# Transposes of the attention probabilities, issued one behind each score matmul instead of in a row

## The reference, cut to what matters

```
scores = (q_nope @ k_nope.T + q_pe @ k_pe.T) * 192 ** -0.5
scores = where(mask, scores, -inf)          # mask: the 128 best causal keys of each query
attn   = softmax(scores, axis=-1)
out    = attn @ v                           # then @ o_w, added to x
```

## Time and profile before

| | us |
|---|---|
| median of 3 runs (896.3 to 898.85) | 897.53 |
| span of the profiled execution | 897.2 |
| first attention pass, about | 300 to 500 of the span |
| second attention pass, about | 500 to 801 of the span |
| a unit of the second pass, from one O to the next | 18.79 |
| PE busy over the span | 805.0 (90%) |
| DVE busy over the span | 675.8 (75%) |

### The profile page before, as it was taken

The page is one execution under the profiler, slowest core; times in us unless marked ns, Lnnn a source line. Parts: engine busy times, 40 slices in busy tenths (PEclk is TensorE's granted clock), DMA queues, the critical chain, the costliest instruction groups (busy, mean ns, idle before and its releaser), DMA issues.

```text
span 897.2 us, 20231 instructions
## 1 busy us (share of the span) xinstructions
PE 805.0 (90%) x7496; PEld 500.7 (56%) x7496; DVE 675.8 (75%) x1557; ACT 596.7 (67%) x1340; POOL 531.0 (59%) x440
## 2 busy tenths in 40 slices
PE   4979989977777988898988899999999999999998
PEld 2445544444344655565555567777767777764443
DVE  5365677789998989999999788888888888861000
ACT  2656789978886878787887676776666767750000
POOL 3185368876884555545545587888878788840000
PEclk9989999999998999999999999999999999999999
DMA  8012211112333444443443288788778777880110
GB/s 254 24 36 74 80 41 54 58 31 85 105 114 89 130 125 115 131 111 111 136 129 105 65 137 167 135 137 155 149 147 147 141 137 152 165 168 15 68 51 32
DMA packets 168786, 96.67 MB, mean 108 GB/s; under 512 B 116720, under 2 KB 142704, under 8 KB 168688
## 3 DMA queue, kind: packets, MB, share of 16 engines
q1 hardware_dynamic: 168688, 95.37, 45.8%
HBM read 36.62 MB, written 6.29 MB: 48 GB/s over the span
## 4 chain that ended last, share of the span: by engine, by line
PE 28%; POOL 22%; DVE 21%; issue 15%; DMA 5%; SPq 4%; ACT 4%; POOLq 0%; DVEq 0%; ACTq 0%
PE psS L773 9%; DVE m L1176 5%; DMA arena<-arena 4%; DVE bias L1183 4%; DVE arena L1042 3%; DVE arena L1236 3%; SPq L451 3%; PE psS L700 3%; PE psT L572 2%; PE psT L552 2%; PE psS L529 2%; POOL arena L1356 2%; POOL arena L1469 2%; POOL bias L1422 2%; ACT arena L804 2%
## 5 line engine op out<-in xcount | busy, mean ns | idle before, releaser
L804 ACT ACTIVATE arena<-psT 128x512 f16<-128x512 f32 (+4 forms) x360 | 171.9, 506 | 107.0 <-PE psT L757 67.1
L700 PE MATMUL psS<-keyT,arena 128*128 128x512 f16 (+3 forms) x1152 | 232.6, 330 | 5.2 <-issue 3.0
L1236 DVE CUSTOM_DVE_ANT_0 arena<-psS,bias 128x512 f32<-128x512 f32 (+7 forms) x256 | 191.9, 751 | 36.7 <-PE psS L700 17.0
L991 ACT ACTIVATE arena<-arena,small 128x512 f32<-128x512 f32 (+7 forms) x256 | 197.5, 774 | 31.0 <-DVE small L1236 30.1
L1042 DVE SCALAR_TENSOR_TENSOR arena<-psT,arena 128x512 f16<-128x512 f32 (+3 forms) x278 | 146.1, 545 | 26.3 <-ACT arena L804 25.7
L757 PE MATMUL psT<-ident,arena 128*128 128x128 f32 x736 | 117.3, 281 | 26.3 <-DVE arena L1042 24.3
L700 PEld LDWEIGHTS psS<-keyT,arena 128*128 128x128 f16 x1152 | 92.6, 99 | 57.1 <-issue 8.1
L585 PE MATMUL psS<-ikT,big 128*128 128x512 f16 (+3 forms) x528 | 102.8, 339 | 23.9 <-DVE bias L1127 20.0
L757 PEld LDWEIGHTS psT<-ident,arena 128*128 128x128 f32 x736 | 86.1, 143 | 59.1 <-ACT arena L991 32.3
L1422 POOL TENSOR_TENSOR bias<-arena,bias 128x768 f32<-128x768 f32 (+2 forms) x48 | 91.4, 1918 | 32.7 <-ACT arena L870 22.3
L1183 DVE MATCH_REPLACE8 bias<-m,bias 128x768 f32<-128x768 f32 (+4 forms) x112 | 89.9, 809 | 0.0
(11 more groups left out here) (164 smaller groups left out, 1387.2 us busy)
## 6 DMA issues: line engine op xcount, KB each, us to landing
arena<-arena SPq DMA_DIRECT2D x192, 128.0 KB, 2.4
arena<-in_wiq SPq DMA_DIRECT2D x32, 256.0 KB, 2.7
arena<-in_ow SPq DMA_DIRECT2D x16, 512.0 KB, 3.5
arena<-in_qbT SPq DMA_DIRECT2D x16, 256.0 KB, 2.5
wvo_parts<-arena SPq DMA_DIRECT2D x16, 256.0 KB, 2.0
arena<-in_qpe SPq DMA_DIRECT2D x16, 128.0 KB, 3.0
arena<-in_x SPq DMA_DIRECT2D x8, 256.0 KB, 3.2
out<-arena SPq DMA_DIRECT2D x8, 256.0 KB, 2.0
```

Of the source, the lines that this page charges most:

```text
L700: last = mm(bank[:, k:k + w], Q[:, u % 2, h, a, q:q + P], keyT[:, b, h, k:k + w], start=(a, b) == (0, 0), stop=(a, b) == (1, 0))
L804: return nc.scalar.activation(dst, src, ACT.Copy, scale=scale)
L991: nc.scalar.activation(pr[:, g % 4, 0:kw], pr[:, g % 4, 0:kw], ACT.Exp, bias=shift[:, g % 4:g % 4 + 1], scale=-1.0, accum_out=rsum[:, unit ...
L1236: v.tensor_tensor_reduce(out=pr[:, g % 4, 0:kw], in0=bank[:, 0:kw], in1=bias[:, TOFF[t]:TOFF[t + 1]], scale=-c_s, scalar=3e38, op0=ALU.add ...
```

## The change

In the second pass, for even steps g that have a step g + 3, the transposes of g are no longer issued in a row behind the six score matmuls of step g + 3. One is issued behind each of these matmuls, and what is left over (3 of 8, none of 5, 1 of 7) follows behind the sixth; of these the first stands behind the score matmul that raises `s_mm`. The waits for `exp_done` and for the two banks of the ring go with the first and the fifth transpose. This holds for 63 steps: four in each of the 16 units, without step 6 of the last one. The first pass keeps its order. The instructions of DVE, ACT, POOL and SP, and their order, stay as they are.

```diff
-            def scores(g):
+            def scores(g, between=None):
 ...
-                last.then_inc(s_mm, 1)
+                        if (a, b) == (1, 0) and k + w == kw:
+                            last.then_inc(s_mm, 1)
+                        if between:
+                            turn_block(between, next(between[1], None))
+
+            def turn_block(step, j):
+
+                if j is None:
+                    return
+                g, nb = step[0], tile_of(step[0]) + 1
+                c = j // 4
+                use = ("T", g, c)
+                if j == 0:
+                    pe.wait_ge(exp_done, g + 1)
+                if j % 4 == 0:
+                    wait_freed(BEFORE[use])
+                last = nc.tensor.transpose(psT[BANK[use]][:, (j % 4) * P:(j % 4 + 1) * P],
+                                           pr[:, g % 4, j * P:(j + 1) * P], ident[:])
+                if j % 4 == 3 or j == nb - 1:
+                    last.then_inc(t_mm, 1)
 ...
             for g in range(STEPS):
+                blocks = iter(range(0 if turns(g) else tile_of(g) + 1))
                 if g + AHEAD < STEPS:
-                    scores(g + AHEAD)
-                if not turns(g):
-                    pe.wait_ge(exp_done, g + 1)
+                    scores(g + AHEAD, (g, blocks) if half_of(g) and not turns(g) else None)
+                for j in blocks:
+                    turn_block((g, blocks), j)
                 for use in uses_of(g):
                     what, at, c = use
                     bank = psT[BANK[use]]
+                    if what == "T":
+                        continue
                     wait_freed(BEFORE[use])
-                    if what == "T":
-                        for j in range(4 * c, min(4 * c + 4, tile_of(g) + 1)):
-                            last = nc.tensor.transpose(bank[:, (j % 4) * P:(j % 4 + 1) * P],
-                                                       pr[:, g % 4, j * P:(j + 1) * P], ident[:])
-                        last.then_inc(t_mm, 1)
-                    elif what == "O":
+                    if what == "O":
```

## The result

The changed kernel takes 910.04 us in the median (909.4 to 911.59), the kernel before 897.39 beside it: a ratio of 1.0146, 95% interval 1.0131 to 1.0161, so 12.6 us slower. The forecast was 908.5, in a range of 899 to 914.

The account below looks back on a forecast made before the run. PE was taken to set the pace, busy 18.65 of 18.79 us a unit. 13 x 0.72 = 9.4, plus 1.1 and 0.55, made 11.0 on a span of 897.2; with 0.3 for the median, 908.5, range 899 to 914.

Parts of the forecast that it names:

- Nothing to win on PE: Transposes between score matmuls on PE: each still costs 0.109 us, as in a row, so alternating is worth nothing.
- `s_mm` late by 0.545: In odd steps `s_mm` comes five transposes later, 5 x 0.109 = 0.545 us, delaying DVE's `row_max` and what queues behind it.
- The hole ahead of O: PE's wait for DVE before O, once a unit: grows from 0.30 to 0.84 us.
- L and the fifth transpose: PE waits 0.18 us at L; step 6's fifth transpose, dependent on DVE's read of L, is due at about that lateness.
- The two waits are one and the same lateness: Step 6's fifth transpose adds no wait beyond L's 0.18 us; the sixth score matmul starts 0.72 later.
- the 13 regular units: Units of the second pass with the full delay: 0.72 us each, 9.4 us together.
- The first unit: First unit of the second pass: taken like the last but one, with only the first step's 0.545 us coming through.
- The three end terms: Second pass's first and last but one units, 1.1 us together, and its last unit, 0.55 us.
- A: Rival for PE: a transpose behind a score matmul costs 0.056 instead of 0.109 us, giving 883 us; chance 0.08.
- C: Rival for PE: each change between fp32 and half precision costs, giving about 930 us, or 915 at a third; chance 0.05.
- B: Rival for DVE: its 3.3 us without work a unit let it catch up, no change, 897.5 us; chance 0.10.
- D: Rival: only one of two latenesses reaches O, a unit loses 0.2 to 0.5 us, giving 901 to 905; chance 0.08.

Follow-up runs that it names:

- e1_steps02: Kernel before, with transposes alternating with score matmuls only in steps 0 and 2 of each unit: 898.41 us, ratio 1.0013.
- e3_step6: Kernel before, with transposes alternating with score matmuls only in step 6 of each unit: 905.55 us, ratio 1.0094.
- e7_two: As e3_step6, but only two transposes stand ahead of the sixth score matmul: 901.40 us, ratio 1.0046 to the kernel before.
- e4_late_signal: Kernel before, transposes in rows, but in steps 4 and 6 the fifth transpose raises `s_mm`: 908.87 us, ratio 1.0124.
- e6_dve_first: As e3_step6, but DVE takes T6a's low part and the read of O ahead of their steps' `row_max`: 894.75 us, 0.9962 to the kernel before.
- e2_step4: Kernel before, with transposes alternating with score matmuls only in step 4 of each unit: 902.09 us, ratio 1.0049.
- e5_O_early: Kernel before, transposes in rows, but O of the second pass issued in step 5 instead of step 7: 896.39 us, ratio 0.9978.
- e8_change_on_e5: The change put on top of e5_O_early, so all even steps alternate and O is in step 5: 922.11 us, 1.0266 to the kernel before.
- e9_dve_first_row: Kernel before, all transposes in rows, with only DVE's order of e6_dve_first: 897.41 us, ratio 0.9982.

## Why the prediction was right

*Nothing to win on PE.* Right, with the value taken: 0.109 a transpose in a row and alternating, shown by e1_steps02.

*`s_mm` late by 0.545, and what hangs on it.* Right. e3_step6 measures 0.55 at O, e7_two 0.22 for two transposes, and e4_late_signal gets 11.0 of 12.6 us from the signal alone. The hole ahead of O was put at 0.84 and is 0.85. That DVE's idle time in a unit does not take up the lateness, because the order of DVE is fixed, is what e6_dve_first shows by changing that order.

*L and the fifth transpose.* L: 0.18 forecast, 0.17 measured. "The two waits are one and the same lateness" was nearly right: the fifth transpose did start on time, but its load had waited for DVE and was not done beneath the score matmul ahead, so it held PE 0.05 longer than its price. That is the difference between 0.72 and 0.77 a unit. The prediction knew this 0.05 from O and had it among its bounds, but left it out here.

*The sum.* From the last O of the first pass to the O of the very last unit it is 506.73 to 800.54 before and 505.13 to 811.42 after, 12.5 us more, against 11.0 forecast. Of this the 13 regular units gave 10.05 (524.79 to 769.27, and 524.65 to 779.18) instead of 9.4. The first unit, up to 524.79 and 524.65, was the term that missed most: 1.46 instead of 0.55. There the first transposes of steps 0 and 4 wait for their banks, ahead of five score matmuls, as DVE is behind at the start of the pass:

```profile
506.67 0.30 PE L718 MATMUL psT<-ident,arena 128*128 128x128 f32 x1 [0.22 <-DVE arena L1059]
...
515.13 0.30 PE L718 MATMUL psT<-ident,arena 128*128 128x128 f32 x1 [0.29 <-DVE arena L1059]
```

I had taken this unit like the last but one without reading it. That one gave 0.84, with such a wait too, and the last unit 0.12 instead of 0.55. The three end terms were off in both directions, 1.65 forecast and 2.42 measured together; that the total is as close as it is rests on the 13 regular units.

*The rivals.* A fell with the price of the single transpose, 0.11 in e1_steps02, and C with the unit of that run, 0.02 longer. B asked for a `row_max` of step 1' behind the low part of T6a; e6_dve_first does just that, and gets it, so B was a condition on DVE's order and not on spare time. D asked for 0.2 to 0.5 a unit, with only one of the two latenesses reaching O; both reach it, 0.18 in e2_step4 and 0.55 in e3_step6.

## What to carry to other kernels

Where an engine works through its queue without gaps, spreading its instructions wins nothing unless the spread ones get cheaper; but every signal at the end of the group that was spread comes later. Look for who sat idle waiting for that signal, and follow that engine's fixed order to the next thing the first engine waits for. And whoever moves instructions moves their waits: a wait that ended early behind a group may keep back the whole group ahead of it, and with it the engine that should end the wait.

## What the runs showed of the hardware that was not expected

The price of a transpose depends on how early its load starts. Behind a score matmul of 512 columns the load starts with that matmul, 0.21 us ahead of the transpose. Where a transpose has to wait, its load starts later, as at 619.77 above and here, in the changed kernel:

```profile
506.64 0.14 PEld L718 LDWEIGHTS psT<-ident,arena 128*128 128x128 f32 x1 [0.49 <-issue]
```

With 0.01 us between the start of the load and that of the transpose (619.77 and 619.78) it is 0.16 to the next start, with 0.03 (506.64 and 506.67) 0.14, with 0.06 (617.14 and 617.20 in e1_steps02) 0.11, and with 0.21 (617.03) 0.11 as well. The first transpose of O, which had to wait too, has a row of 0.33 (622.54) where a transpose behind 512 columns has 0.27, and O's four take 0.49 instead of 0.44, before and after. In e5_O_early O does not wait, but the value matmul ahead of it gives its load only 0.03, and the four take 0.47. So a load that starts with its transpose costs some 0.05, and 0.06 us of other work ahead hide nearly all of it.

In the profiled run of the changed kernel the granted clock of TensorE was 0.66 over 5 us of the output stage, so part of that time it was at the lower of its two levels, 1.2 GHz; this came after a wait of 2.0 us, which the kernel before has too, without the fall. Two windows, and PE there:

```profile
838.60:843.60 5.00, 4.96 (x16) 1.91 (x17) 0.58 (x1) 0.00 (x0) 0.00 (x0) 0.66 0.62 211
840.60:841.60 1.00, 1.00 (x3) 0.29 (x2) 0.00 (x0) 0.00 (x0) 0.00 (x0) 0.50 0.81 291
```

```profile
838.64 4.03 PE L790 MATMUL psS<-w1hi,big 128*128 128x512 f16 x12 [2.01 <-DVE arena L1345]
```

Twelve matmuls took 4.03 us where other such rows take 2.75. From the last O to DVE's last instruction that execution took 70.56 us (836.02 to 906.58) instead of 68.87 (825.15 to 894.02): 1.7 us, and no part of the 12.5 of the pass. Up to the last O of the first pass it was 1.6 faster (505.13 against 506.73), so the two spans differ by 12.6 all the same. The fall is no matter of the change alone: the profiled executions of e3_step6, e6_dve_first, e8_change_on_e5 and e9_dve_first_row have the same 0.66 over 5 us there, those of the other six experiments and of the kernel before 1.00.
